# Attention stage: the per-batch fronts moved ahead of the loop, halves swapped by DMA, both score pairs of a step together

## The reference

```python
cq  = gelu(x @ wq + bq);  ckv = gelu(x @ wkv + bkv)        # "latent", 64 channels each
q_c = cq @ wqc + bqc;     k_c = ckv @ wkc + bkc            # 128 channels: heads 0 to 7
q_r = rope(x @ wqr + bqr); k_r = rope(x @ wkr + bkr)       # 128 channels: heads 8 to 15
v   = ckv @ wv + bv
q   = gelu(concat(q_c, q_r)); k = gelu(concat(k_c, k_r))
out = softmax(causal(q @ k.T / 4)) @ v @ wo + bo           # x is the layer-normed residual
# rope(x) = x * cos + concat(-x2, x1) * sin,  x1, x2 the halves of the 128 channels
```

## Time and profile before

| | us |
|---|---|
| median of 3 runs | 5140.43 (5124.07 to 5151.45) |
| the profiled execution | 5133.93, of which span 5132.2 |
| attention stage: first DMA issue to first score matmul | 3717.4 to 3854.1 |
| attention stage: loop | 3854.1 to 4714.6 |
| last projections | 4714.6 to 4728.0 |

### The profile page before, as it was taken

How to read it: one execution, slowest core, us unless ns; L and a number is a source line. 1 busy time by engine, 2 the same in 40 slices (tenths; PEclk the granted TensorE clock), 3 DMA queues, 4 the chain that set the end, 5 groups by cost and what they waited for, 6 DMA issues and landing times.

```text
span 5132.2 us, 49428 instructions
## 1 busy us (share of the span) xinstructions
PE 3978.6 (78%) x15218; PEld 2283.6 (44%) x15218; DVE 2808.6 (55%) x4916; ACT 2304.2 (45%) x4166; POOL 2539.4 (49%) x2184
## 2 busy tenths in 40 slices
PE   6888878769948777996778699948937777788892
PEld 2333333357715455773333356645712323233571
DVE  6999999841156663114888822255244545454422
ACT  5566656321157663113555333332525555555241
POOL 6999999722222333114889644423552424222256
PEclk8999999869969887997888799969957878889896
DMA  5666666512110001223555411150532404221145
GB/s 151 160 156 161 161 160 155 149 42 96 64 50 17 33 25 57 82 78 103 150 153 144 137 43 45 45 158 20 149 87 52 79 19 70 38 39 39 51 130 133
DMA packets 310841, 472.53 MB, mean 92 GB/s; under 512 B 34634, under 2 KB 167734, under 8 KB 310506
## 3 DMA queue, kind: packets, MB, share of 16 engines
q1 hardware_dynamic: 277152, 388.87, 28.9%
q0 software_dynamic: 29184, 76.12, 5.3%
q10 hardware_dynamic: 4224, 4.19, 0.2%
HBM read 375.26 MB, written 97.49 MB: 92 GB/s over the span
## 4 chain that ended last, share of the span: by engine, by line
PE 39%; DVE 6%; POOL 6%; ACT 5%; issue 5%; DMA 3%; SPq 0%; another core or an unknown queue 0%; DVEq 0%; POOLq 0%; ACTq 0%
PE s_gate_up L2305 7%; PE s_result_sum L2321 4%; PE s_out_sum L3632 3%; PE s_hidden_sum L1745 3%; PE s_result_sum L1756 3%; PE s_scores_T L3616 2%; POOL s_h L435 2%; PE s_shared L2961 2%; DVE s_maxima L3272 2%; PE s_scores L3577 2%; PE s_shared L2971 1%; PE s_transposed L2295 1%; POOL s_gathered L1047 1%; POOL s_h L444 1%; DMA s_bc<-s_bc_rows 1%
## 5 line engine op out<-in xcount | busy, mean ns | idle before, releaser
L435 POOL TENSOR_TENSOR s_h<-s_dtu,s_bc 128x1024 f32<-128x1024 f32 x384 | 904.2, 2363 | 73.0 <-PE s_y_sum L477 54.1
L477 PE MATMUL s_y_sum<-s_h,identity 128*128 128x512 f32 x1536 | 770.3, 639 | 160.5 <-POOL s_h L444 151.5
L402 ACT ACTIVATE s_decay<-s_dt,s_A 128x512 f32<-128x512 f32 x768 | 498.4, 682 | 330.3 <-DVE s_h L377 323.3
L477 PEld LDWEIGHTS s_y_sum<-s_h,identity 128*128 128x128 f32 x1536 | 295.0, 202 | 599.2 <-issue 302.4
L3430 ACT ACTIVATE s_weights_T<-s_scores_T 128x1024 f32<-128x1024 f32 (+3 forms) x384 | 302.9, 810 | 369.9 <-PE s_scores_T L3616 364.7
L3272 DVE TENSOR_REDUCE s_maxima<-s_scores 128x1 f32<-128x512 f32 (+3 forms) x438 | 279.0, 659 | 318.0 <-PE s_scores L3580 223.3
L2305 PE MATMUL s_gate_up<-s_w_gate_up,s_rowsT 128*128 x1184 | 420.8, 488 | 3.2 <-issue 2.5
L444 POOL TENSOR_TENSOR s_h<-s_h,s_bc 128x512 f32<-128x512 f32 x288 | 367.0, 1275 | 23.4 <-DVE s_h L370 15.5
L2364 DVE TENSOR_TENSOR s_mid<-s_act,s_gate_up 128x128 f32<-128x128 f32 (+1 forms) x228 | 92.9, 408 | 455.4 <-ACT s_act L2337 433.1
L3492 POOL TENSOR_SCALAR_AFFINE_SELECT s_weights_T<-s_weights_T 128x256 f32<-128x256 f32 x256 | 104.3, 412 | 458.6 <-ACT s_weights_T L3430 457.3
L370 DVE TENSOR_TENSOR_SCAN s_decay<-s_decay,s_carry,s_h 128x512 f32<-128x512 f32 x240 | 303.4, 1278 | 24.3 <-POOL s_clip_flag L2633 13.9
(11 more groups left out here) (525 smaller groups left out, 7989.9 us busy)
## 6 DMA issues: line engine op xcount, KB each, us to landing
s_bc<-s_bc_rows SPq DMA_DIRECT2D x384, 512.0 KB, 4.9
sorted_results<-s_result SPq DMA_DIRECT2D x160, 128.0 KB
s_w_inter<-in_L_ffn_experts_inter SPq DMA_DIRECT2D x16, 1024.0 KB
s_w_exp_out<-in_L_ffn_experts_out SPq DMA_DIRECT2D x16, 1024.0 KB
s_queries<-parts_of_q SPq DMA_DIRECT2D x96, 128.0 KB
s_keys<-parts_of_k SPq DMA_DIRECT2D x96, 128.0 KB
results_by_token<-zeros SPq DMA_DIRECT2D x16, 512.0 KB, 6.1
s_pair<-results_by_token SPq DMA_DIRECT2D x16, 512.0 KB, 6.8
```

The costliest lines, as they stand in the source:

```text
L402: S.e.activation(self.decay[:, (2 * g + d) % 4, :], dt[q // self.passes % 2][:, at, :], ACT.Exp, scale=A[:, at, g % ns:g % ns + 1]).then_i ...
L435: G.e.tensor_tensor(self.h[r][:], dtu[q // self.passes % 2][:, at:at + 2, :], mid(self.bc[r][:, 0, :], 2), ALU.mult).then_inc(*self.fed.up())
L477: made = T.e.matmul(self.y[:, d, :], ident[:], self.h[r][:, d, :], start=False, stop=g % ns == ns - 1)
```

## The change

The diff has four parts. In its core below, `cross` is VectorE's, `rests` GpSimd's (VectorE's for tile (1, 0)), the two `dma_start` ScalarE's (in `rotate`), the last lines TensorE's `main`.

1. **A head.** All four fronts are issued by a new schedule, `head`, with 21 ticks for each batch (`PERIOD`), before the loop. It also holds the first 61 maxima pieces of unit 0 and its values. `program` starts at u = 0 and has only maxima, highest, values, projection and bias. `head_is_over` makes VectorE and ScalarE wait for the last three stagings, because the loop's buffers lie in the head's memory. The combine ring has 4 tiles instead of 2. The parts of all units have places of their own in DRAM; the SBUF parts are a ring of 3.
2. **The rotary part.** The ScalarE copies of the halves become two DMAs from ScalarE's queue. The products with cos and sin and their sum move from GpSimd to VectorE.
3. **The split** writes its second remainder as the third part: 2 casts and 2 subtractions in place of 3 and 2. Tile (1, 0), the rotary queries, is subtracted on VectorE, the other three on GpSimd.
4. **A step** is `scores(n, 0)`, `scores(n, 1)`, side work of both ticks, `product(n - 2)`. `FIRST` is 10 instead of 14, so `EARLY` is 23 instead of 16.

```diff
-    combine = Combine(K, M, X, 2, 1)
+    combine = Combine(K, H, X, 4, 1)
-    FIRST = 14
+    PERIOD, HEAD_MAX, HEAD_VALUES = 21, 62, (112, 114)
+    GATHER, SUM, STATS, FACTORS = (-4, -2, 0, 2, 5, 8, 10, 12), (4, 6, 8, 9, 11, 13, 15, 18), (10, 19), (13, 20)
+    NORM, TURN, TURNED = ((14, 15), (21, 22)), ((16, 17), (24, 25)), ((17, 18), (25, 26))
+    LATENT, LATENT_MADE, CONTENT, CONTENT_MADE = (20, 31), (21, 32), ((23, 24), (34, 35)), ((25, 26), (35, 36))
+    ROTATE, ROTATED, CROSS, ROTARY_MADE = ((28, 30), (36, 38)), ((29, 31), (37, 39)), (35, 43), (39, 47)
+    SPLIT = (((36, 38, 40, 42), (38, 40, 42, 45)), ((41, 44, 45, 49), (48, 50, 52, 54)))
+    FIRST = 10
+    def head(**side):
+        work = [("setup", 0)]
+        for b in range(NB):
+            work += [(n, b) for n in ("gathers", "sums", "stats", "factors", "norm", "turn", "turned_rows", "latents",
+                                      "content", "rotate", "cross", "rotary")]
+            work += [("split", (b, ct, j)) for ct in range(DT) for j in range(2)]
+        work += [("highest", (0, 0)), ("maxima", (0, 0, False)), ("maxima", (0, 1, False)), ("values", 0)]
+        sides = [Side(side[n](i)) for n, i in work if n in side]
+        for tick in range(-PERIOD, PERIOD * NB + TICKS):
+            for s in sides:
+                s.until(tick)
...
-        for u in range(-3, n_units + 1):
+        for u in range(n_units + 1):
...
+        def cross(b):
+            for j in range(2):
+                yield PERIOD * b + CROSS[j]
+                V.wait_ge(*weights_here.now())
+                V.wait_ge(*swapped.at(2 * b + j))
+                for i, (to, table) in enumerate(((act[1][j], cos), (crossed, sin))):
+                    V.e.tensor_tensor(to[:], to[:], table[:], ALU.mult).then_inc(*v_step.up())
+                    yield PERIOD * b + CROSS[j] + i + 1
+                V.wait_ge(*v_step.now())
+                V.e.tensor_tensor(act[1][j][:], act[1][j][:], crossed[:], ALU.add).then_inc(*rope_added.up())
+    def rests(E, v):
+        b, ct, j = v
+        to = parts[(4 * b + 2 * ct + j) % 3]
+        yield PERIOD * b + SPLIT[ct][j][1]
+        E.wait_ge(*cast0[ct][j].at(b))
+        E.e.tensor_tensor(act[ct][j][:], act[ct][j][:], to[:, 0, :], ALU.subtract).then_inc(*rest[ct][j].up())
+        yield PERIOD * b + SPLIT[ct][j][3]
+        E.wait_ge(*cast1[ct][j].at(b))
+        E.e.tensor_tensor(to[:, 2, :], act[ct][j][:], to[:, 1, :], ALU.subtract).then_inc(*split_done[ct][j].up())
+    def head_is_over(E):
+        for i in range(2 * n_units - 3, 2 * n_units):
+            E.wait_ge(*staged[i % 3].at(i // 3))
...
+                S.wait_ge(*roped.now())
+                S.wait_ge(*rope_added.at(2 * b + j - 1))
+                for half in range(2):
+                    S.e.dma_start(crossed[half * DC:(half + 1) * DC, :],
+                                  act[1][j][(1 - half) * DC:(2 - half) * DC, :]).then_inc(*swapped.dma())
...
                     scores(n, 0)
+                    scores(n, 1)
                 beside(2 * s)
-                if n < N_STEPS:
-                    scores(n, 1)
```

More of the change, by code:

```diff
@@ L3112, in projects @@
         return range(u // DT * PAIRS - 2, u // DT * PAIRS) if u > 0 else ()
-    def ropes(u, j):
-        made = u + (2 if j else 3)
-        return made if 0 < made < n_units and made % DT else 0
     B = Banks()
-    for u in range(-3, n_units + 1):
+    B.of["bv"], B.of["max", 0, 0] = 7, 4
+    for i in range(2):
+        B.of["values", 0, i] = 3 + i
+    for a, n in ((0, PER), (1, EARLY)):
+        for i in range(n):
+            B.of["scores", 0, a, i] = 1 + i % 2
+    for u in range(n_units + 1):
@@ L3143, in attention_stage @@
-        B.place(pieces, [2 * s + 1 for s in range(NS) if ends(NS * u + s - 3)])
+        if u + 1 < n_units:
+            pieces += [(value_tick(u + 1, i), value_tick(u + 1, i) + 1, ("values", u + 1, i)) for i in range(2)]
+        for a in range(2):
+            if u + 1 - a < n_units:
+                pieces.append((max_tick(u + 1 - a, a), max_tick(u + 1 - a, a) + 1, ("max", u + 1 - a, a)))
+        for v, a, some in ((u, 1, range(EARLY, PER)), (u + 1, 0, range(PER)), (u + 1, 1, range(EARLY))):
+            if v < n_units:
+                pieces += [(score_tick(v, a, i), score_tick(v, a, i), ("scores", v, a, i)) for i in some]
@@ L3177, in beside @@
                     s.until(tick)
-            if u >= 0:
-                main(u, beside)
-            for tick in range(TICKS):
-                beside(tick)
+            main(u, beside)
             beside(WHOLE)
@@ L3493, in main, with take @@
                 beside(2 * s + 1)
-        program(main, combine=sums, front=front, rope=rope, split=split, bias=bias)
+        head(gathers=gathers, factors=factors, split=split)
+        program(main, bias=bias)
     def tensor():
         T.wait_ge(*prepared.at(0))
-        free = [turned.at(-1)] * 3
-        ob_free = [turned.at(-1)]
-        def take(name, until):
-            f = B.of[name]
+        free = [turned.at(-1)] * len(bank)
+        def take(f, until):
             T.wait_ge(*free[f])
@@ L3660, in main @@
                     product(n - 2)
-        program(main, setup=setup, values=values, front=front, rotate=rotate, maxima=maxima, highest=highest, project=project)
+        head(setup=setup, turn=turn, latents=latents, content=content, rotate=rotate, maxima=maxima, highest=highest,
+             values=values)
+        program(main, values=values, maxima=maxima, highest=highest, project=project)
     sync()
```

462 lines of the change are left out of this document (219 added, 243 removed).

## The result

The kernel after takes 5054.2 us (median of 4 runs, 5048.4 to 5058.8) against 5135.3 (5124.1 to 5151.5) of the kernel before on the same chip: ratio 0.9839, 95% interval 0.9809 to 0.9869. That is 81 us less. The forecast was 4956 (range 4900 to 5030): the direction was right, the gain 45% of the 179 us between 5135.3 and 4956, and the time outside the range. The profiled execution took 5048.4 us.

A forecast was written before the change was run, and what follows sets the result against it. TensorE paces the loop, slowed by the fronts; GpSimd's queue sets the new head. From 5133.9 us, head +48 (185 against 136.7) and loop -233 (627.5 against 860.5) give 4949, or 4956 on the median; range 4900 to 5030.

The forecast's parts named there:

- that gather is issued some 121 us after the start: Head: GpSimd issues the last batch's last gather after 64 gathers, 6 factors (11.6 us) and 12 subtractions (25.6 us).
- the 30 that the prediction named as a sign of being wrong: Head: the forecast is wrong if GpSimd waits for rings or casts by more than some 30 us.
- 80%: Head: sign of being right, GpSimd busy near 80% of it.
- the 8 of collisions: Head: 8 us added for VectorE and GpSimd operations meeting and slowing each other.
- the batches do not overlap: Head, rival: each batch takes its own chain, head 383 us, result 5154; chance 0.04.
- The last batch's chain: Head: steps one after another behind the last gather's issue, together 55 us, first exponential 177 us after the start.
- 8.2 each: Head, last batch's chain: a swap and its three VectorE operations, done twice, 16.4 us.
- GpSimd and VectorE exclude each other: Head, rival: 70 us of two-input VectorE work lie in GpSimd's queue, head 265 us, result 5036; chance 0.10.
- The tail: Head, end of the last batch's chain: only a staging of 4.5 us before the first exponential.
- unit 6 is the sample: Loop: unit 6, with no front beside it, shows what units become; units 1 to 6 start from 87.5 us.
- the 4.5 us taken off for clock and pairing: Loop, units 1 to 6: 2 us for pairing and 2.5 for clock, giving 83 us a unit.
- the second rival: Loop: paired scores wait for exponentials or side work clumps, units of 95 us, result 5040; chance 0.09.

The follow-up runs named there:

- Early_chain: Kernel after with gathers, sums, statistics and factors of each batch eight ticks earlier: 5043.7 us, head 236.8.
- spread: Kernel after with unit 0 stacked behind batch 1's stagings, unit 1 last, unit 0's maxima from tick 84, aggregations ahead of rotary products: 5042.2 us, ratio 0.9816.
- early_spread: Kernel after with both the eight-tick-earlier first links and the later stacking, later maxima and earlier aggregations: 5026.1 us, ratio 0.9780, head 231.6.
- unpaired: Kernel after with the scores of a step's pairs apart again, side work between them: 5050.3 us, ratio 0.9861, loop 672.4.
- first14: Kernel after with FIRST back at 14 in place of 10: 5056.2 us, loop 663.0.
- Before_paired: Kernel before with only the pairing of a step's scores, one line moved in TensorE's list: 5096.5 us, ratio 0.9923.
- Half_sums: early_spread72 without the second matmul of each latent sum and rotary projection in the head: 5041.9 us, head 241.0.
- copies: Kernel after with two ScalarE copies in place of a tile's two swap DMAs: 5039.1 us, ratio 0.985, head 254.0.
- no_rope: Kernel after without the rotation (swaps, products with cos and sin, their sum): 5012.7 us, head 226.3.
- early_spread72: early_spread with unit 0's maxima from tick 72 in place of 84: 5036.2 us, ratio 0.9792, head 241.4.

## Why the prediction was wrong

**What failed: "that gather is issued some 121 us after the start".** It was issued at 168.5 us, and the last factors ended at 195.6, not 133. The working added GpSimd's instructions up to there and let none of them wait. In fact GpSimd waits inside each batch, up to the last gather 24 us for VectorE's aggregation and 16 for ScalarE's casts, up to the last factors 37.7 and 19.1. Over the whole head the waits for casts alone are 41 us, above the 30 that the prediction named as a sign of being wrong, and GpSimd was busy 55% of the head and not 80%. Each wait holds the gathers of a later batch, whose sums the same queue waits for again. Early_chain changes this order and gives back 18 to 22 us; spread takes stacking and maxima off the chain and gives 8 to 12; both together 23 to 27. With both, in early_spread, the last gather is issued at 129 us, near the 121 of the forecast: these two, the order of the queues and the place of stacking and maxima, are what made it late.

By the terms of the sum the head's 69 us are: 63 up to the last factors (195.6 for 132.8), 8 in the chain behind them (47.1 for 38.7 without the staging), 7 in the tail (11.5 for 4.5), together 78; less the 8 of collisions that the forecast had as a term of their own, and 1 of its rounding. This sum says where the time stood, not what a cure gives: in early_spread the last factors are within 13 us of the forecast (146 for 133), but some 22 us then stand in the chain behind them and 20 in the tail, so 47 of the 69 us are still there.

The prediction named the mechanism as a rival (*the batches do not overlap*), but only in its whole form, 383 us. Half of it happened: two batches in flight, not one. It should have been priced in between, as 121 plus the waits of one ring. The burst of stackings and the late staging were in no term and no rival.

**The last batch's chain** behind the factors was sized 8 us short: 47.1 us to the last split. The rotation took 10.7 and 12.3 us (3936.4 to 3947.1 and to 3959.4) against 8.2 each. A swap landed 4 to 5 us after its issue (forecast 4.5). Three of VectorE's six operations were stretched, as its timeline shows, against GpSimd's at the same time:

```profile
3943.24 2.78 POOL L3368 TENSOR_TENSOR s_act0q<-s_act0q,s_parts 128x1024 f32<-128x1024 f32 x1 [5.32 <-ACT s_parts L3452]
3945.98 3.11 POOL L3368 TENSOR_TENSOR s_act0k<-s_act0k,s_parts 128x1024 f32<-128x1024 f32 x1
```

```profile
3942.82 1.21 DVE L3288 TENSOR_TENSOR s_crossed<-s_crossed,s_sin 128x1024 f32<-128x1024 f32 x1
...
3944.56 2.54 DVE L3291 TENSOR_TENSOR s_act1q<-s_act1q,s_crossed 128x1024 f32<-128x1024 f32 x1
...
3954.16 2.54 DVE L3288 TENSOR_TENSOR s_crossed<-s_crossed,s_sin 128x1024 f32<-128x1024 f32 x1
```

**GpSimd and VectorE exclude each other** was right in kind and small in sum. One of VectorE's products takes 2.54 us where another takes 1.21, and one of GpSimd's subtractions 3.11 where 2.12 is usual. Over the head VectorE's adds have a mean of 593 ns against the 484 usual, 7 us for 64; the large operations add some 5 us, and GpSimd's 24 subtractions lost 4 (four of them took 2.8 to 3.2 us). No run takes this term alone out of the head; as a sum of busy times 12 us on VectorE and 4 on GpSimd are near the 8 taken and far from the rival's 70. The rows show the turns: VectorE's L3291 begins at 3944.56 and ends at 3947.10, about one usual length behind the end of GpSimd's L3368 at 3946.02, and GpSimd's next one ends about one usual length behind that. The rule of the Trainium skill (SBUF — State Buffer, "Who interferes with whom") is that the first to come has the shared port for its whole instruction and the other stands; these rows agree with it. The sum is small because few meet: of VectorE's 96 two-input operations 12 ran at the same time as a subtraction of GpSimd's. The 35 adds beside gathers alone took 485 ns, as usual.

**The tail** between the last split (3967.7) and the first exponential is not the staging, issued at 3967.75. PE went on with the last maxima pieces until 3976.8, and then ScalarE loaded its table for 1.28 us (3977.98). The table load was in no term.

**The loop.** The idea that unit 6 is the sample held: units of 85.6 to 88.4 us against its 87.5. Unit 0 (78.5 for 78) and unit 7 (52.6 for 51.5) were right. Of the 4.5 us taken off for clock and pairing nothing is left in the length: the mean is 87.1 for 83, six times 4 us. PE's busy time fell by 3 us as expected, from 75.3 to 70 to 73 with a clock of 0.94 to 0.98, but its idle time rose from 12.2 to 15. Its waits by releaser in unit 6 after:

```profile
L3617 PE MATMUL s_scores<-s_keys,s_queries 96*128 96x512 bf16 (+3 forms) x67 | 19.9, 338 | 4.0 <-DVE s_maxima L3308 2.2 <-ACT s_out_channels L3471 0.9 <-DVE s_max_parts L3327 0.7
L3617 PE MATMUL s_misc<-s_keys,s_queries 96*128 96x512 bf16 (+3 forms) x29 | 8.9, 339 | 5.2 <-DVE s_out_rows L3347 4.2 <-DVE s_max_parts L3327 0.7 <-ACT s_values L3462 0.2
L3686 PE MATMUL s_misc<-identity,s_out_T 128*128 128x128 f32 x16 | 2.5, 278 | 2.4 <-DVE s_maxima L3308 2.4
```

The waits for ScalarE fell as forecast, 2.9 to 0.9 and 1.6 to 0.2 us. In their place stand waits for VectorE: in unit 6 they are 13.6 us for 7.8 before, 5.6 for 5.1 of them at the evicted output rows and 4.8 for 1.6 at maxima. I had priced only ScalarE; that side work clumps stood in the second rival. The pairing, which puts side work in one lump, is one part of the rise: unpaired has 11.3 us there. `FIRST` = 10 seems to be another: first14 has 11.0. The rest is open. Unpaired suggests that the pairing still pays, some 2 us a unit, through less busy time of PE at a higher granted clock and not through less idle time; why the clock was higher is not shown. Before_paired shows more (47 us of the loop, 38 of the time), where the fronts' copies on ScalarE are in the way as well. The effects do not add: on the moved fronts the pairing gives 5 to 19 us.

**Where the gain went**, then: the loop gave 207 us, of the 233 forecast, and the head took 115 back (251.8 us to the first score matmul, for 136.7), not 48. With 7.6 us more ahead of the stage and 1.5 less behind the loop that makes the 85.6 us between the two spans.

What stays open: the 47 us behind the last factors, why they grow to 61 when the factors come sooner, and the 74 us of batch 0 alone. Half_sums excludes the time of two of TensorE's sums, copies the way of swapping, no_rope gives the rotation a share. That the rest is the alternation of casts and subtractions is only argued, from the timeline.

## What to carry over

- A queue's sum is a floor, not a forecast, when its instructions wait for engines that wait for it. Write down for each engine which instruction of batch b stands ahead of which of batch b + 2, look for a ring, and count how many batches can be in flight.
- Before moving an instruction earlier in an in-order queue, see when its data land: early_spread72 lost 10 us in the head because a matmul stood 24 us with the last batch behind it.
- Run the small part of a change alone: here one moved call gave half of the gain. And before reading a few us out of a stage, see how far unchanged code differs: here by up to 14 us in the loop.

## What was not expected of the hardware

Less work on TensorE bought no time and a lower clock: 16 us less of busy time in the same 241 us, and 0.59 granted in place of 0.66 (one profile each). And stacking in one burst has a price elsewhere: one staging issued into it landed after 15.8 us, and after 18.6 in two other runs, where 3.5 to 5 are usual.
